# The gates of an mLSTM attention layer, computed with tokens on the partitions instead of gates on the rows

## The reference

```
q = layernorm(x);  k = v = ctx_1024
ig = [q,k,v] @ w_igate.T + b_igate          # per head and token
fg = [q,k,v] @ w_fgate.T + b_fgate
log_f = log_sigmoid(fg);  pcs = cumsum(log_f) over tokens
log_D[s,t] = pcs[s] - pcs[t] + ig[t]  for t <= s, else -inf
m[s] = max over t of log_D[s,t];  D = exp(log_D - m)
C = (q k^T / sqrt(128)) * D
h = C / (max(|sum_t C|, exp(-m)) + 1e-6) @ v
x = x + tanh(g_xattn) * headnorm(h) * (1 + ln_weight)
x = x + tanh(g_ffn) * moe(layernorm(x))     # top 2 of 8, capacity 1075, gelu(x W1 + b1) W2 + b2
```

## Time and profile before

| | |
|---|---|
| median of 3 runs | 2086.83 us |
| span of the profiled execution | 2081.7 us |
| the profiled execution's own time | not given; the page has its span only |
| busy share of the span, PE / DVE / ACT / POOL | 93% / 40% / 34% / 17% |
| attention part | to about 400 us |
| choice of experts and first weights | about 400 to 470 us |
| experts | from about 470 us |
| one slot, between the head statistics of two batches | 44 us |

### The profile page before, as it was taken

The page is one execution under the profiler, slowest core; times in us unless marked ns, Lnnn a source line. Parts: engine busy times, 40 slices in busy tenths (PEclk is TensorE's granted clock), DMA queues, the critical chain, the costliest instruction groups (busy, mean ns, idle before and its releaser), DMA issues.

```text
span 2081.7 us, 28147 instructions
## 1 busy us (share of the span) xinstructions
PE 1928.8 (93%) x10037; PEld 1636.3 (79%) x10037; DVE 836.9 (40%) x1879; ACT 713.2 (34%) x1447; POOL 357.9 (17%) x296
## 2 busy tenths in 40 slices
PE   5888888249999999999999999999999999999996
PEld 3555555148888888888888888888888888888885
DVE  4898987771224223512342143214322422242121
ACT  3444443312235223422442243224322532352221
POOL 1222233552100111011101111101110111001100
PEclk9999999679999999999999999999999999999998
DMA  4334532611104212411340133014310431041111
GB/s 139 102 122 154 164 128 102 201 61 55 29 10 141 75 29 50 139 36 29 78 128 20 29 99 112 20 25 118 107 22 10 138 84 29 14 137 34 29 15 14
DMA packets 104507, 157.53 MB, mean 76 GB/s; under 512 B 6912, under 2 KB 56192, under 8 KB 103376
## 3 DMA queue, kind: packets, MB, share of 16 engines
q1 hardware_dynamic: 88272, 120.54, 17.3%
q0 software_dynamic: 16128, 35.41, 9.4%
HBM read 120.85 MB, written 35.06 MB: 75 GB/s over the span
## 4 chain that ended last, share of the span: by engine, by line
PE 80%; DVE 13%; issue 2%; DMA 2%; ACT 1%; POOL 1%; DVEq 0%; POOLq 0%; ACTq 0%
PE PS L813 38%; PE PS L800 36%; DVE stats L1046 2%; PE PS L675 2%; PE PS L783 1%; DVE heads L1144 1%; DVE decay L1104 1%; DVE stats L1117 1%; PE PS L651 1%; DMA out_dram<-y_out,rows_add 1%; PE PS L666 1%; DVE g_max L1083 1%; DVE qn L1056 1%; DMA negmax<-negmax_rows 1%; DVE g_cum L1081 0%
## 5 line engine op out<-in xcount | busy, mean ns | idle before, releaser
L1312 DVE TENSOR_TENSOR h_lo<-h_raw,h_hi 128x360 fp32r<-128x360 f32 x384 | 205.1, 534 | 1081.8 <-ACT h_hi L1006 1076.1
L1005 ACT ACTIVATE h_raw<-PS,b_now 128x360 f32<-128x360 f32 x384 | 215.8, 562 | 1046.1 <-PE PS L800 1033.8
L800 PE MATMUL PS<-x_hi,w_hi 128*128 128x360 f32 x1536 | 504.1, 328 | 2.3 <-DVE x_lo L1299 1.3
L800 PE MATMUL PS<-x_hi,w_lo 128*128 128x360 f32 x1536 | 503.5, 328 | 0.0
L800 PE MATMUL PS<-x_lo,w_hi 128*128 128x360 f32 x1536 | 501.5, 326 | 0.0
L813 PE MATMUL PS<-w_hi,h_hi 128*120 128x512 f32 x1152 | 459.7, 399 | 0.0
L813 PE MATMUL PS<-w_lo,h_hi 128*120 128x512 f32 x1152 | 453.7, 394 | 0.0
L813 PE MATMUL PS<-w_hi,h_lo 128*120 128x512 f32 x1152 | 453.1, 393 | 0.0
L586 POOL DMA_INDIRECT out_dram<-y_out,rows_add x72 | 124.0, 1722 | 1341.9 <-DVE y_out L1340 1127.5
L800 PEld LDWEIGHTS PS<-x_hi,w_hi 128*128 128x128 f32 x1536 | 289.5, 188 | 24.2 <-issue 3.1
L800 PEld LDWEIGHTS PS<-x_lo,w_hi 128*128 128x128 f32 x1536 | 289.3, 188 | 16.4
(11 more groups left out here) (160 smaller groups left out, 1468.2 us busy)
## 6 DMA issues: line engine op xcount, KB each, us to landing
raw<-in_L_ffn_W_dram SPq DMA_DIRECT2D x128, 512.0 KB
x_front<-in_x_dram SPq DMA_DIRECT2D x8, 1024.0 KB, 7.0
vs<-in_ctx_dram SPq DMA_DIRECT2D x32, 256.0 KB, 4.6
negmax<-negmax_rows SPq DMA_DIRECT2D x8, 1024.0 KB, 4.7
x_back<-in_x_dram SPq DMA_DIRECT2D x8, 1024.0 KB, 8.9
out_dram<-x_back SPq DMA_DIRECT2D x8, 1024.0 KB, 4.4
xn_rows<-xn SPq DMA_DIRECT2D x8, 1024.0 KB, 5.2
b_row<-in_L_ffn_b_dram SPq DMA_DIRECT2D x8, 256.0 KB, 4.2
```

Source lines behind the costliest of these rows:

```text
L800: ins = T.matmul(PS[:, HB + n % 3, 0:CW], w[:, w_at(j), k * P:(k + 1) * P], v[:, c, k, :], start=(k == 0 and a == 0), stop=(k == KT - 1 an ...
L1005: A.activation(h_raw[:, n % 3, :], PS[:, HB + n % 3, 0:CW], ACT.Gelu, bias=b1_now[:, n % HT:n % HT + 1])
L1312: V.tensor_tensor(h_lo[:, n % 3, :], h_raw[:, n % 3, :], h_hi[:, n % 3, :].bitcast(F32), ALU.subtract)\
```

## The change

The gates get their tokens on the partitions. `gate_products` swaps its operands: the transposed queries and context become the stationary side (128 columns of tokens), the gate weights the moving side (8 columns), for 4 tiles of tokens and 8 tiles of features, so that PSUM holds 128 partitions by 4 tiles by 8 gates. Bias, absolute value and minimum work on 128 partitions by 32 or 16 columns. The running sum over tokens becomes a product with a triangle of ones within a tile and with ones for the tiles before (`gate_sums`, four products). g is then a column at once (`gate_columns`), and PE turns it into a row (`turn_gates`) for the one thing that stays a row, the running maximum (`gate_maxima`). It reads PSUM and goes to DRAM with its sign kept; the decays' exponentials take scale -1. PE turns the maxima into columns (`turn_maxima`) and DVE adds the sums (`gate_tops`).

In the queues: on DVE `gates_first` now stands ahead of `front_norm`, the end of `gates_second` is split into four parts at four places. On PE `gate_sums` stands between `scores(b,2)` and `outputs(b,1)`, `turn_gates` behind `outputs(b,1)`, `turn_maxima` where `gate_columns` stood. The products of the next batch wait for `top_made` instead of `gates_taken`. The constants of the gates lie in 8 rows, the biases are read to all 128 partitions, and two fills on POOL are gone for one triangle. Renamed buffers and semaphores are left out below.

```diff
-GR = 36
+GR = 2 * NH
...
-        gate_bias = sb("gate_bias", [GR, 1], F32, a_mem)
+        gate_bias = sb("gate_bias", [P, GR], F32, a_mem)
+        not_after = sb("not_after", [P, P], F32, a_mem)
...
-        g_f = sb("g_f", [NH, S], F32, a_mem)
-        g_i = sb("g_i", [NH, S], F32, a_mem)
-        g_t = sb("g_t", [NH, S], F32, a_mem)
-        g_cum = sb("g_cum", [NH, S], F32, a_mem)
+        g_pre = sb("g_pre", [P, ST, GR], F32, a_mem)
+        g_t = sb("g_t", [P, ST, NH], F32, a_mem)
+        g_log = sb("g_log", [P, ST, NH], F32, a_mem)
+        g_cum = sb("g_cum", [P, ST, NH], F32, a_mem)
...
-        cols_ps = PS[:, GATE, 0:ST * GR].rearrange("p (t g) -> p t g", t=ST)
+        gates_ps = PS[:, GATE, 0:ST * GR].rearrange("p (t g) -> p t g", t=ST)
+        sums_ps = PS[:, GATE, 32:32 + ST * NH].rearrange("p (t h) -> p t h", t=ST)
+        max_ps = PS[:, GATE, 64:64 + ST * NH].rearrange("p (t h) -> p t h", t=ST)
...
-            sp.dma_start(gate_bias[0:NH, :], b_fg.rearrange("(h o) -> h o", o=1)).then_inc(const_in, 16)
-            sp.dma_start(gate_bias[32:32 + NH, :], b_ig.rearrange("(h o) -> h o", o=1)).then_inc(const_in, 16)
+            sp.dma_start(wload[NH:GR, :], w_ig).then_inc(const_in, 16)
+            sp.dma_start(gate_bias[:, 0:NH], b_fg.partition_broadcast(P)).then_inc(const_in, 16)
+            sp.dma_start(gate_bias[:, NH:GR], b_ig.partition_broadcast(P)).then_inc(const_in, 16)
...
-            G.memset(wload[:, :], 0.0)
...
-            G.memset(g_rows[:, :], 0.0)
+            G.affine_select(out=not_after[:, :], in_=ones[:, 0:P], compare_op=ALU.is_ge, fill=0.0, base=0,
+                            pattern=[[1, P]], channel_multiplier=-1)
...
-                wait_past(pe, gates_taken, at(b, 1, 0))
+                wait_past(pe, top_made, at(b, 1, 0))
                 if b[1] >= 2:
                     pe.wait_ge(back_copied, START + at(b, 4, -8))
-                for k in range(2 * KT):
-                    src = qT[p][:, k, :] if k < KT else kT[p][:, k - KT, :]
-                    ins = T.matmul(PS[0:GR, GATE, :], wgate[:, k, :], src, start=(k == 0), stop=(k == 2 * KT - 1))
+                for t in range(ST):
+                    for k in range(2 * KT):
+                        src = (qT[p] if k < KT else kT[p])[:, k % KT, t * P:(t + 1) * P]
+                        ins = T.matmul(gates_ps[:, t, :], src, wgate[:, k, :], start=(k == 0), stop=(k == 2 * KT - 1))
                 ins.then_inc(gates_made, 1)
 
-            def gate_columns(b):
-                wait_apart(pe, gate_rows_made, at(b, 1, 1))
-                wait_apart(pe, cols_copied, at(b, 1, 0))
+            def gate_sums(b):
+
+                pe.wait_ge(logs_made, at(b, 1, 1))
+                T.matmul(sums_ps, not_after[:, :], g_log[:, :, :], start=True, stop=False)
+                for t in range(ST - 1):
+                    earlier = g_log[:, t:t + 1, :].to_broadcast([P, ST - 1 - t, NH])
+                    ins = T.matmul(sums_ps[:, t + 1:ST, :], ones[:, 0:P], earlier, start=False, stop=(t == ST - 2))
+                ins.then_inc(sums_made, 1)
+
+            def turn_gates(b):
+
+                pe.wait_ge(cols_made, at(b, 1, 1))
                 for t in range(ST):
-                    ins = T.transpose(cols_ps[:, t, :], g_rows[:, t * P:(t + 1) * P], ident[0:GR, 0:GR])
-                ins.then_inc(cols_made, 1)
+                    ins = T.transpose(PS[0:NH, GATE, t * P:(t + 1) * P], cols[b[1] % 2][:, t, :], ident[:, :])
+                ins.then_inc(rows_made, 1)
+
+            def turn_maxima(b):
+
+                wait_apart(pe, max_made, at(b, 1, 1))
+                for t in range(ST):
+                    ins = T.transpose(max_ps[:, t, :], g_max[:, t * P:(t + 1) * P], ident[0:NH, 0:NH])
+                ins.then_inc(max_turned, 1)
...
+                if there(front):
+                    gate_sums(front)
+                if there(b):
                     outputs(b, 1)
+                if there(front):
+                    turn_gates(front)
...
-                    gate_columns(front)
+                    turn_maxima(front)
...
-            def exp_negmax(b):
-                act.wait_ge(cols_copied, at(b, 1, 1))
+            def exp_top(b):
+                act.wait_ge(top_made, at(b, 1, 1))
                 wait_past(act, x1_made, START + at(b, 1, -1))
-                A.activation(expneg[b[1] % 2][:, :, :], cols[b[1] % 2][:, :, 32:32 + NH], ACT.Exp).then_inc(expneg_made, 1)
+                A.activation(expneg[b[1] % 2][:, :, :], top_log[b[1] % 2][:, :, :], ACT.Exp, scale=-1.0).then_inc(expneg_made, 1)
...
-                    ins = A.activation(decay[h % 2][:, t, t * P:S], negmax[p][:, h, t * P:S], ACT.Exp,
-                                       bias=cols[p][:, t, h:h + 1])
+                    ins = A.activation(decay[h % 2][:, t, t * P:S], maxima[p][:, h, t * P:S], ACT.Exp,
+                                       bias=cols[p][:, t, h:h + 1], scale=-1.0)
...
-                gates = PS[:, GATE, :]
-                V.tensor_scalar(g_f[:, :], gates[0:NH, :], gate_bias[0:NH, 0:1], None, ALU.add)
-                chain(V.tensor_scalar(g_i[:, :], gates[32:32 + NH, :], gate_bias[32:32 + NH, 0:1], None, ALU.add))
-                dve.sem_inc(gates_taken, 1)
-                V.scalar_tensor_tensor(g_t[:, :], g_f[:, :], -1.0, g_f[:, :], ALU.mult, ALU.max).then_inc(abs_made, 1)
-
-            def gates_second(b, chain):
+                bias = gate_bias[:, :].rearrange("p (o g) -> p o g", o=1).to_broadcast([P, ST, GR])
+                chain(V.tensor_tensor(g_pre[:, :, :], gates_ps, bias, ALU.add))
+                f = g_pre[:, :, 0:NH]
+                V.scalar_tensor_tensor(g_t[:, :, :], f, -1.0, f, ALU.mult, ALU.max).then_inc(abs_made, 1)
+
+            def gate_logs(b):
                 dve.wait_ge(softplus_made, at(b, 1, 1))
-
-                chain(V.scalar_tensor_tensor(g_f[:, :], g_f[:, :], 0.0, g_t[:, :], ALU.min, ALU.subtract))
-                chain(V.tensor_tensor_scan(g_cum[:, :], ones[0:NH, :], g_f[:, :], 0.0, ALU.mult, ALU.add))
-                chain(V.tensor_tensor(g_i[:, :], g_i[:, :], g_cum[:, :], ALU.subtract))
-                chain(V.tensor_tensor_scan(g_max[:, :], ones[0:NH, :], g_i[:, :], LOWEST, ALU.mult, ALU.max))
-                wait_past(dve, negrow_out, at(b, 16, 0))
-                wait_past(dve, cols_made, at(b, 1, 0))
-                V.tensor_scalar(g_neg[:, :], g_max[:, :], -1.0, None, ALU.mult).then_inc(negrow_made, 1)
-                V.tensor_copy(g_rows[0:NH, :], g_i[:, :])
-
-                V.scalar_tensor_tensor(g_rows[32:32 + NH, :], g_cum[:, :], -1.0, g_max[:, :], ALU.mult, ALU.subtract)\
-                    .then_inc(gate_rows_made, 1)
+                V.scalar_tensor_tensor(g_log[:, :, :], g_pre[:, :, 0:NH], 0.0, g_t[:, :, :], ALU.min, ALU.subtract)\
+                    .then_inc(logs_made, 1)
 
             def gate_columns(b):
+                dve.wait_ge(sums_made, at(b, 1, 1))
+                wait_past(dve, decay_made, at(b, 4, -4))
+                V.tensor_copy(g_cum[:, :, :], sums_ps)
+                V.tensor_tensor(cols[b[1] % 2][:, :, :], g_pre[:, :, NH:GR], sums_ps, ALU.subtract).then_inc(cols_made, 1)
+
+            def gate_maxima(b):
+                dve.wait_ge(rows_made, at(b, 1, 1))
+                wait_past(dve, max_out, at(b, 16, 0))
+                V.tensor_tensor_scan(g_max[:, :], ones[0:NH, :], PS[0:NH, GATE, :], LOWEST, ALU.mult, ALU.max).then_inc(max_made, 1)
+
+            def gate_tops(b):
+                dve.wait_ge(max_turned, at(b, 1, 1))
                 dve.wait_ge(cols_made, at(b, 1, 1))
-                wait_past(dve, decay_made, at(b, 4, -4))
                 wait_past(dve, expneg_made, at(b, 1, -1))
-                V.tensor_copy(cols[b[1] % 2][:, :, :], cols_ps).then_inc(cols_copied, 1)
+                V.tensor_tensor(top_log[b[1] % 2][:, :, :], g_cum[:, :, :], max_ps, ALU.add).then_inc(top_made, 1)
...
                     front_stats(ahead, chain)
+                if there(front):
+                    gates_first(front, chain)
+                if there(ahead):
                     front_norm(ahead, chain)
                 if there(front):
-                    gates_first(front, chain)
+                    gate_logs(front)
                 if there(b):
                     weigh(b, 2)
                 if there(front):
-                    gates_second(front, chain)
+                    gate_columns(front)
                 if there(back):
                     second_stats(back, chain)
+                if there(front):
+                    gate_maxima(front)
                 if there(b):
                     weigh(b, 3)
                 if there(front):
-                    gate_columns(front)
+                    gate_tops(front)
                 if there(back):
                     second_norm(back, chain)
                 if there(last):
```

(55 more changed lines are left out.)

1 line of the change is left out of this document (removed).

## The result

The changed kernel takes 2116.61 us (median of 4 runs, 2111.99 to 2120.13) beside 2086.52 for the kernel before (4 runs, 2083.64 to 2087.01): the ratio is 1.0152 with an interval of 1.0138 to 1.0165, slower by 30 us. The forecast was 2074, the range 2064 to 2104; the time lies above both. The span went from 2081.7 to 2118.4 us. That is 36.7 us and not 30, because the profiled executions are not the median ones: that of the kernel after took 2120.13 us, 3.5 above its median, and that of the kernel before some 3.1 under its own (an estimate: the span and the 1.7 us by which every run here is longer than its span).

A forecast was written before the change was run, and what follows sets the result against it. DVE's queue sets the slot, PE close behind. Savings 6.3 (batch 1) + 4 x 2.8 (router slots) - 4 (clock falls) + 0.3 (constants) - 0.5 (batch 6) = 13.3 us, giving 2074; own range 2064 to 2083, with rivals 2064 to 2104.

The forecast's parts named there:

- the swap of operands is free at full clock: Gate products on PE: 64 load-and-matmul pairs would take 7.0 us, where 16 wide instructions took 7.06.
- Rival one: TensorE's clock falls within the gate products; half the pairs slow gives 10.5 us of products, 2093 in all; chance 0.42.
- batch 1: Slot without a router: the forecast saved 6.3 us; with half the pairs slow it still gains 3.5.
- batch 6: Slot with no load ahead, DVE and PE both waiting at the gates: loses 0.5 us, or 5.7 under the clock fall.
- no gain: Four router slots with half the pairs slow: slot ends at about 251.5 us; the forecast saved 2.8 us each.
- the filling: Pipeline start, first gates to row leaving: again 7 to 8.5 us, counted as nothing; the clock fall costs 3.7 and 0.7.
- the rival's worst case: All gate pairs at half speed: products 14 us, the slots lose some 2 us each, 2106 us in all.
- DVE's wait for the products: With gates_first ahead of front_norm, DVE is ready at about 225.0 and products end at 228.7: 3.7 us.
- wait for the logs: PE idles 2.3 us after scores(2); the clock may then fall, counted in two of four slots at 2 us.
- Newton chain: Small DVE instructions held at 1.02 to 1.19 us while POOL's residual runs, 0.16 otherwise; the chain cannot end before the residual.
- the 5.1 us that the prediction puts around the span: Difference between the profiled span, 2081.7 us, and the runs' median, 2086.83; both were to move alike.
- Rival two: Gate pairs cost only 0.058 us, PE waits 4.7 us for the logs, the clock falls each time: 2080; chance 0.12.
- Rival three: DVE's added wait is the whole story and slots keep their length: around 2086; no share of its own.

The follow-up runs named there:

- 64 columns and the same order: The changed kernel with zeros behind the 8 gate columns, so each gate product moves 64 columns; 2079.56 us (one run).
- 8 columns and the old place on DVE: The changed kernel, still 8 moving columns, with DVE's front_norm ahead of gates_first again, as before the change; 2102.42 us.
- 64 columns and the old place on DVE: The changed kernel with gate products zero-padded to 64 moving columns and DVE's front_norm ahead of gates_first again; 2076.66 us, ratio 0.9959 to the kernel before.
- moving two steps: The changed kernel with 64 moving columns, on PE the sums behind outputs(1) and the turn behind the router; 2066.12 us, ratio 0.9913 to the kernel before.

## Why the prediction was wrong

**The step that failed** is "the forecast is that the swap of operands is free at full clock", and with it the choice of 7.0 us for the products: the price of a pair was right (0.11 us at full clock), the clock did not hold. Rival one had the mechanism and the place, with a chance of 0.42. The Trainium skill says in "TensorE: Matmul & The Clock Gate", part "The HAM clock gate", that activity releases the throttle. The trace does not bear it out for these loads: the products above have the weight path full, and the clock fell in them all the same.

The price of the pair stands as forecast. The Trainium skill, on the same page, section "LDWEIGHTS (loading the stationary operand)", gives 107 ns for 128 columns, an estimate from its rule; the runs agree at full clock, 0.112 us a pair, and not at the low level, 0.213.

**What rival one mis-sized.** It said 6.6 us slower, the profiled spans 36.7. Some of its terms were right: batch 1 gains 4.2 (3.5), batch 6 loses 5.5 (5.7), and in one of the four slots with a router the products take 10.7 us (10.5), outputs(1) are back at 2.48, and the slot is 44.3 us long, the "no gain" of the rival. In the other three the products last 10.8 to 12.8 us. In two of the three the low stretch also goes on past scores(2), the one step that the rival priced behind them, through the sums (1.57 for 1.0) and outputs(1) (4.01 for 2.3). These slots are 47.7 to 49.2 us, and the four together lose 12.5 where the rival had 0. The largest miss is the filling: the rival gave the first two gates 3.7 and 0.7 us, and it lost 18.9. With 64 columns and the same order it loses 3.0 (78.27 for 75.31), so some 16 of it hang on the clock; with 8 columns and the old place on DVE it loses 7.9, so the new place makes the low clock dearer there. The last slot and the rest of the span add 1.7 and 2.3, which had not been counted. Even the rival's worst case, 2106 with all pairs at half speed and 14 us a batch, stayed under the 2116.6, though the products took 11.6 us on average, so the pairs alone do not account for it. In the filling the two sets of products are 11.3 us longer than before, and the other 7.6 lie between and behind them. The forecast's range left even that case out.

**What was right**, in the kernel with 64 columns, which is the forecast's own case: products 7.2 us (7.0), DVE's wait for the products 4.13 (3.7), wait for the logs 2.26 (2.3), a fall behind it in two of four slots at 1.7 to 2.2 us (two at 2), outputs(3) at 2.49, Newton chain at 0.16 once the residual is over, scan 1.21 (1.5, lower end 1.2). Beside the residual the bias add takes 0.19 us, and the absolute value is held to 0.86, as forecast. (Of the four instructions of the Newton chain that were held before, the one of L1040 reads a single tensor, and it was held as long as the others, 1.20 us: two inputs are not what they share.) That the falls are two is luck: with the old place on DVE it is three of the four. This kernel still took 2079.6 for 2074. Its span is 3.9 us shorter than before, where 13.3 were forecast. The missing 9.4 are: 3.3 in the filling (first statistics at 78.27, forecast 75.0), of which the new order is 2.9; 3.5 in the slots (281.4 us to the last statistics, forecast 277.9); 2.6 behind them, where nothing was counted and the kernels of the new form lose 0.3 to 3.2; the cause was not looked for. No row stands behind the 0.3 us that the sum takes for the earlier constants; the first products start at 21.88 here and at 22.21 in the changed kernel, where they started at 22.24. And the 5.1 us that the prediction puts around the span are 1.7 in every run here; the rest is that the profiled execution was faster than the median. The forecast is the median less 13.3 all the same.

**The order of PE** the prediction took as given. It named the wait and its cost and stopped there; moving two steps was worth 13.4 us. That is what it had counted for them: the waits were 9.1 us in the four slots with a router (2.54, 2.17, 2.26, 2.16) and the two falls some 4.

**Rival two** (cheap loads, 0.058 a pair) fell: 0.112. **Rival three** fell as well: with 64 columns the added wait on DVE is 4.13 us and the kernel is faster than before.

## To carry to other kernels

Price a swap of operands at both levels of TensorE's clock, with all the work behind it until the clock is seen at 1.00 again, and where a stretch of loads with few moving columns stands alone, try the same stretch with zeros added to the moving side: here it gave back 37 us, at the same 0.11 us a pair. Read the granted clock of such a stretch, not its busy share, which was 12.56 of 12.60 us here. When a wait for a short result stands in the queue of the engine that becomes the bound, put ready work ahead of it.

## What was not expected of the hardware

- A pair of a 128-column load and a matmul takes 0.112 us at full clock with 8, 32, 64 or 128 moving columns; with 8, in two kernels of quite different order, and with 32 in one, TensorE fell to 1.2 GHz some 1 to 4 us into the pairs, with 64 and 128 it stayed at 2.4 GHz.
- PE idle 2.26 us, after dense work, was followed by outputs of 4.12 us instead of 2.40, and idle of 2.16 us by outputs of 2.48. The length does not decide it: with 64 columns and the old place on DVE, 2.08 us was followed by 4.01 and 2.18 by 2.48. So a wait of this length costs nothing or some 2 us, and the rows before it do not tell which.
- The running maximum reads its row out of PSUM in 1.21 us, where the scans out of SBUF had taken 1.2 to 1.5 in the kernel before.
